# A Flamingo-style two-layer kernel: the second half's router and shared-expert tasks stand one unit later, and the last block of expert weights is split behind the routing-weight chain

## The chip, the cores and the metric

The kernel runs on one core of one Trainium2 chip. The metric is the device time of one execution in microseconds (us). For the kernel before, three timed runs gave 567.09, 568.3 and 570.09 us; the median is 568.3 us. Engines are named as the profile names them: PE (TensorE, matmuls), PEld (its weight loads), DVE (VectorE), ACT (ScalarE), POOL (GpSimd) and SP (SyncE, which issues the DMAs).

## The reference, cut to what matters

Four sub-layers stand one after another on 1024 tokens of width 256. The change touches only the last one, the routed experts:

```python
logits = x @ gate_w.T                       # 32 experts
scores = sigmoid(logits); sb = scores + gate_bias
# groups of 8 experts: the two best groups stay, then the 8 best experts of those
wsel = wsel / wsel.sum(-1, keepdims=True) * 2.5          # routing weights cw
x_lat = x @ fc1_w.T                                      # 256 -> 128
h = relu2(einsum('tl,eil->eti', x_lat, w1)) * cw.T[:, :, None]
y_lat = einsum('eti,eli->tl', h, w2)
routed = y_lat @ fc2_w.T
shared = relu2(x @ shared_up_w.T) @ shared_down_w.T
out = x_in + tanh(g_ffn[1]) * (shared + routed)
```

## The kernel before, in words

Every product is computed as three matmuls (lo by hi, hi by lo, hi by hi), so that every operand exists as a "hi" tile, a rounded copy that ACT writes, and a "lo" tile, the remainder that DVE or POOL subtracts. Whatever feeds PE therefore passes through ACT and then DVE or POOL.

The 1024 tokens are two halves of 512. The experts run as 64 units, `i` from 0 to 63: units 0 to 31 are the 32 experts on the first half of the tokens, 32 to 63 the same experts on the second half. In unit `i` PE runs `down(i)` and then `up(i + 4)`, a "pair" of six 128x512 matmuls. Between `up` and `down` of one unit DVE multiplies relu by the row of routing weights (`root`, tile `e_r`), ACT squares it (`expert_square`, tiles `e_hi` and `e_sq` or a PSUM bank), and DVE or POOL subtracts (`expert_low`, tile `e_lo`). POOL takes the subtraction in units 1, 3, 6, 8, 10, 12, 27, 29 and 31 of the first half.

While the first half's experts run, the second half's normalisation, router, latent projection and shared expert are computed by single "tasks", each put ahead of one unit's pair by the table `TASK_IN_UNIT`. `N` transposes one 128-row chunk of the normalised tokens `h` (two tasks; ACT then writes `hT_hi`, DVE `hT_lo`), `L` computes the logits (24 matmuls of 32 columns), `X` the latent projection, `U` a quarter of the shared expert's up projection (four tasks), `C` transposes the finished routing weights `cw`. All tasks use PSUM bank 1, so each waits until the one before it has been read out (`wait_taken`). The order on every engine is the order in which the code issues it; nothing reorders it. The places of the router's own steps are written as unit numbers too: `scores_of_experts`, `best_of_groups`, `best_experts`, `weight_sum` on DVE, and `biased`, `mask_groups`, `choose`, `roots_begin`, `roots_step`, `roots_end` on POOL. Together they make the chain from `L` to `C`; `roots_end` writes `cw` and signals `cw_ready`.

Expert weights arrive in blocks of 4 experts (128x1024). SP loads a block, ACT copies its hi part (`block_high`, placed by `UNIT_OF_BLOCK`), POOL subtracts its lo part (`block_low`, placed by `LOW_UNIT_OF_BLOCK`), and PE waits for `blk_done` ahead of the first `up` that uses it. Block 28 serves experts 12 to 15, block 29 experts 16 to 19, block 30 experts 20 to 23, block 31 experts 24 to 27 and block 32, the last, experts 28 to 31 (tiles `ex_hi1`, `ex_lo1`); so `up(28)`, which stands in unit 24, needs block 32.

After `C` the weights go through ACT (`cwT`) to DRAM and come back as rows (`store_weights`, `load_row`) for the second half's `root(32)` and on.

Of the kernel before, what the change touches and what calls it, by code (L numbers as in the profile page):

```python
# [5 lines left out]
def flamingo_two_layer_kernel(nc, x, ids, ctx_t, g_xattn, g_ffn, w_gate_t, w_up_t, w_down_t,  # L6
# [19 lines left out]
    NG = 2  # L26
# [11 lines left out]
    SC = SI // P  # L38
# [11 lines left out]
    with ctx:  # L50
# [169 lines left out]
        for q in (2, 3):  # L220
# [81 lines left out]
                  ("K", 3), ("V", 3), ("S", 0), ("D", 0)] + [("E", q) for q in range(E // 4)]  # L302
        STEP_OF_BLOCK = {0: 10, 1: 11, 2: 12, 3: 13, 4: 14, 5: 15, 7: 16, 8: 17, 9: 18, 11: 19, 12: 20, 13: 21, 15: 22,
                         22: 23, 24: 24, 27: 25, 30: 26, 31: 27}
        UNIT_OF_BLOCK = {0: 28, 6: 29, 7: 30, 10: 31, 16: 32}
        LOW_UNIT_OF_BLOCK = {1: 28, 6: 29, 7: 30, 10: 31, 16: 32}
        LOAD_AT_ROW = {4: 29, 8: 30, 13: 31, 16: 32}


        TASK_IN_STEP = {"m11": ("M", 0), "e11": ("M", 1), "e22": ("N", 0), "m23": ("N", 1), "e23": ("L", 0), "m24": ("X", 0),  # L310
                        "e24": ("U", 0), "m25": ("U", 1), "e25": ("U", 2), "m26": ("U", 3), "e30": ("C", 0)}
        TASK_IN_UNIT = {6: ("N", 0), 8: ("N", 1), 10: ("L", 0), 11: ("X", 0), 13: ("U", 0), 15: ("U", 1), 17: ("U", 2), 19: ("U", 3),
                        23: ("C", 0)}
        SHARED_DOWN = {3: (0, 0), 4: (0, 1), 5: (0, 2), 9: (0, 3), 61: (1, 0), 62: (1, 1), 63: (1, 2)}


# [246 lines left out]
        def _(pool):  # L563
# [96 lines left out]
            def shared_low(n):  # L660
                pool.wait_ge(su_taken, n + 1)
                nc.gpsimd.tensor_tensor(s_lo[:, n % SC, :], s_sq[:, n % 2, :], s_hi[:, n % SC, :].bitcast(F32), ALU.subtract)\
                    .then_inc(s_done, 1)
# [67 lines left out]
            def roots_step():  # L731
                own(newton(cwv[:, :], cwy[:, :], cwt[:, :]))

            def roots_end():
                G.tensor_tensor(cw_flat, cw_flat, cwy[:, :], ALU.mult).then_inc(cw_ready, 1)
# [49 lines left out]
            for i in range(NI):  # L785
                expert_low(i + 2)
                if i == 3:
                    norm_factors(1, 3)
                elif i == 11:
                    biased(1)  # L790
                elif i == 13:
                    mask_groups(1)
                elif i == 15:
                    choose(1)
                elif i == 17:
                    roots_begin(1)
                    roots_step()
                elif i == 18:
                    roots_step()
                elif i == 19:  # L800
                    roots_step()
                    roots_end()
                if i in (15, 17, 19, 21):
                    shared_low(SC + (i - 15) // 2)
                if i in LOW_UNIT_OF_BLOCK:
                    block_low(LOW_UNIT_OF_BLOCK[i])

        @block.scalar
        def _(act):
# [245 lines left out]
            for i in range(NI):  # L1055
                expert_square(i + 3)
                if i in TASK_IN_UNIT:
                    take_task(1, TASK_IN_UNIT[i], 1)
                if i in (15, 17, 19, 21):
                    shared_high(SC + (i - 15) // 2)  # L1060
                if i == E + 1:
                    act.wait_ge(down_done, E)
                    nc.scalar.activation(yl_hi[0][:, :], ps[:, 0, :], ACT.Copy).then_inc(yl_hi_done, 2)
                if i in UNIT_OF_BLOCK:
                    block_high(UNIT_OF_BLOCK[i])
# [6 lines left out]
        def _(dve):  # L1072
# [426 lines left out]
                if i >= 1:  # L1499
                    expert_low(i - 1)  # L1500
            for i in range(NI):
                if i in (7, 9):
                    norm_chunk_low(1, (i - 7) // 2, 1, 2 * NG + 4 + (i - 7) // 2)
                elif i == 12:
                    latent_low(1, 1)
                elif i in (14, 16, 18, 20):
                    shared_relu(SC + (i - 14) // 2, 1)
                root(i + 3)
                expert_low(i + 2)
                if i == 0:  # L1510
                    add_attention(GN)
                    add_attention(GN + 1)
                elif i == 1:
                    add_attention(GN + 2)
                    add_attention(GN + 3)
                    count(GN)
                    count(GN + 1)
                elif i == 2:
                    count(GN + 2)
                    own(count(GN + 3))  # L1520
                    aggregate(1)
                elif i == 4:
                    normalise(2, range(GN, GN + 2))
                elif i == 5:
                    normalise(2, range(GN + 2, NT)).then_inc(h_ready, 1)
                elif i == 11:
                    scores_of_experts(1)
                elif i == 12:
                    best_of_groups(1, range(GN)).then_inc(gtop_done, 1)
                elif i == 15:  # L1530
                    best_experts(1)
                elif i == 17:
                    weight_sum(1)
                elif i == E + 2:
                    routed_low(0, 0)
                    routed_low(0, 1)
                elif i == E + 5:
                    add_result(0)
                    add_result(1)
                elif i == E + 6:  # L1540
                    add_result(2)
                    add_result(3)
# [530 lines left out]
```

## Time and profile before

| what | value |
|---|---|
| timed runs | 567.09, 568.3, 570.09 us; median 568.3 us |
| profiled execution, its own time | 568.33 us |
| its span | 566.5 us |
| PE busy | 537.0 us, 95% of the span |
| DVE, ACT, POOL busy | 389.8, 350.9, 320.5 us |
| granted TensorE clock, mean | 0.994 of full speed |

The profiled execution took as long as the median run. Its span, first to last instruction, is 1.8 us shorter than its time. All times below that are points in time are microseconds from the span's start. The stretch that the change touches is 440 to 516 us.

### The profile page before, as it was taken

How to read it: one execution, taken by the hardware profiler on the slowest of the kernel's cores; microseconds unless marked ns; L12 is line 12 of the kernel's file. 1: busy time of each engine (PE TensorE's matmuls, PEld its weight loads, DVE VectorE, ACT ScalarE, POOL GpSimd, SP SyncE). 2: the span in 40 equal slices, each digit the busy share in tenths (PEclk: the TensorE clock that was granted, in tenths of full speed). 3: DMA queues.
4: the chain of work that ended last, by engine and by line, in shares of the span. 5: the costliest groups of instructions: out<-in, count | busy, mean ns of one | idle time of the engine just before them, and what ended most of it. 6: DMA issues, size and time to landing. Idle time of an engine off the chain costs nothing.

```text
span 566.5 us, 9626 instructions
## 1 busy us (share of the span) xinstructions
PE 537.0 (95%) x3240; PEld 462.2 (82%) x3240; DVE 389.8 (69%) x822; ACT 350.9 (62%) x723; POOL 320.5 (57%) x320
## 2 busy tenths in 40 slices
PE   3999998998999999999999999999999989999997
PEld 3877766777778988999999999989998878777786
DVE  4867988689956575656655576646665757878883
ACT  3651155666478676766757565745757665777882
POOL 2579137999348797655544424426698465762220
PEclk9999999999999999999999999989999998999999
DMA  8901136510057768677696768534354735356651
GB/s 278 357 23 46 47 111 185 189 38 1 20 185 226 222 186 261 218 247 224 217 289 191 244 206 229 188 98 163 115 189 149 241 125 174 112 146 189 217 178 39
DMA packets 66672, 95.78 MB, mean 169 GB/s; under 512 B 6336, under 2 KB 38848, under 8 KB 66624
## 3 DMA queue, kind: packets, MB, share of 16 engines
q1 hardware_dynamic: 66624, 95.17, 53.0%
q8 instruction: 27, 0.44, 0.3%
q14 instruction: 21, 0.17, 0.1%
HBM read 67.23 MB, written 27.92 MB: 168 GB/s over the span
## 4 chain that ended last, share of the span: by engine, by line
PE 69%; DVE 11%; POOL 6%; ACT 5%; issue 4%; DMA 3%; SPq 1%; DVEq 0%; POOLq 0%
PE ps L1557 20%; PE ps L1558 19%; PE ps L1559 19%; PE ps L1662 4%; PE ps L1767 2%; PE ps L1751 2%; DMA k_hl<-k_scratch 1%; DVE e_r L1472 1%; PE ps L1774 1%; DMA blk_raw<-in_w_blocks 1%; DVE qtok L1223 1%; ACT q2T L921 1%; PE ps L1780 1%; DMA cw_row<-cw_scratch 1%; DVE e_lo L1482 1%
## 5 line engine op out<-in xcount | busy, mean ns | idle before, releaser
L657 POOL TENSOR_TENSOR probs<-probs,rsum 128x512 f32<-128x512 f32 x64 | 66.4, 1041 | 60.5 <-DVE rsum L1252 60.4
L1247 DVE TENSOR_REDUCE nmax<-ps 128x2 f32<-128x512 f32 x64 | 44.0, 688 | 35.6 <-PE ps L1559 35.3
L959 ACT ACTIVATE probs<-ps,nmax 128x256 f32<-128x256 f32 x128 | 59.7, 481 | 1.6 <-DVE nmax L1247 1.4
L578 POOL TENSOR_TENSOR kv_w_lo<-blk_raw,kv_w_hi 128x1024 fp32r<-128x1024 f32 x16 | 38.9, 2431 | 37.2 <-ACT kv_w_hi L826 37.2
L1045 ACT ACTIVATE e_hi<-e_r 128x512 fp32r<-128x512 f32 x64 | 40.2, 629 | 30.4 <-DVE e_r L1472 29.6
L1472 DVE SCALAR_TENSOR_TENSOR e_r<-ps,cw_row 128x512 f32<-128x512 f32 x64 | 43.6, 684 | 12.8 <-PE ps L1559 10.3
L1238 DVE TENSOR_TENSOR pT_lo<-ps,pT_hi 128x512 fp32r<-128x512 f32 x64 | 43.7, 685 | 11.9 <-ACT pT_hi L965 11.4
L780 POOL TENSOR_TENSOR e_lo<-e_sq,e_hi 128x512 fp32r<-128x512 f32 x19 | 24.5, 1292 | 45.1 <-ACT e_sq L1051 42.6
L1243 DVE TENSOR_TENSOR oT_lo<-ps,oT_hi 128x512 fp32r<-128x512 f32 x32 | 22.1, 691 | 40.2 <-ACT oT_hi L969 40.2
L965 ACT ACTIVATE pT_hi<-ps 128x512 fp32r<-128x512 f32 x64 | 38.3, 600 | 15.9 <-PE ps L1662 15.8
L969 ACT ACTIVATE oT_hi<-ps 128x512 fp32r<-128x512 f32 x32 | 19.1, 597 | 40.8 <-PE ps L1559 40.8
L584 POOL TENSOR_TENSOR k_hl<-k_hl 128x512 fp32r<-128x512 f32 x18 | 23.8, 1322 | 32.1 <-ACT k_hl L894 32.1
L1662 PE MATMUL ps<-eye,probs 128*128 128x128 f32 x256 | 39.0, 275 | 1.6 <-DVE kv_out L1278 1.0
L837 ACT ACTIVATE kv_hi<-ps 128x512 fp32r<-128x512 f32 x38 | 22.9, 602 | 26.9 <-PE ps L1559 26.9
L1557 PE MATMUL ps<-pT_hi,v_hl 128*128 128x256 f32 x128 | 36.6, 286 | 1.1 <-DVE pT_lo L1238 0.5
L1557 PE MATMUL ps<-k_hl,qT_lo 128*128 128x256 f32 x128 | 37.3, 292 | 0.0
L1559 PE MATMUL ps<-k_hl,qT_hi 128*128 128x256 f32 x128 | 36.4, 285 | 0.0
L1558 PE MATMUL ps<-k_hl,qT_hi 128*128 128x256 f32 x128 | 36.3, 284 | 0.0
L1559 PE MATMUL ps<-wo_hi,oT_hi 128*128 128x256 f32 x128 | 36.2, 283 | 0.0
L1558 PE MATMUL ps<-wo_lo,oT_hi 128*128 128x256 f32 x128 | 36.2, 283 | 0.0
L1557 PE MATMUL ps<-wo_hi,oT_lo 128*128 128x256 f32 x128 | 36.2, 283 | 0.0
L1559 PE MATMUL ps<-pT_hi,v_hl 128*128 128x256 f32 x128 | 36.2, 282 | 0.0
(299 smaller groups left out, 1876.9 us busy)
## 6 DMA issues: line engine op xcount, KB each, us to landing
cw_row<-cw_scratch SPq DMA_DIRECT2D x64, 256.0 KB, 3.6
v_hl<-v_scratch SPq DMA_DIRECT2D x24, 512.0 KB, 3.6
blk_raw<-in_w_blocks SPq DMA_DIRECT2D x23, 512.0 KB, 4.4
k_scratch<-kv_out SPq DMA_DIRECT2D x32, 256.0 KB, 2.6
v_scratch<-kv_out SPq DMA_DIRECT2D x32, 256.0 KB, 3.2
k_hl<-k_scratch SPq DMA_DIRECT2D x14, 512.0 KB, 3.5
v_scratch<-kv_hi SPq DMA_DIRECT2D x24, 256.0 KB, 2.8
blk_raw<-in_w_tail SPq DMA_DIRECT2D x10, 512.0 KB, 4.6
```

Of the source, the lines that this page charges most:

```text
L578: nc.gpsimd.tensor_tensor(lo[:, :], blk_raw[j % 2][:, :], hi[:, :].bitcast(F32), ALU.subtract).then_inc(blk_done, 1)
L657: nc.gpsimd.tensor_tensor(probs[:, b, :, :], probs[:, b, :, :], rsum[:, b, :].unsqueeze(2).to_broadcast([P, 2, S]), ALU.mult).then_inc(pro ...
L959: last = nc.scalar.activation(probs[:, b, t, :], ps[:, S_BANK[b], t * S:(t + 1) * S], ACT.Exp, bias=nmax[:, b, t:t + 1], accum_out=esum[:, ...
L965: nc.scalar.activation(pT_hi[:, b, :, :].rearrange("p k q -> p (k q)"), ps[:, P_BANK[b], :], ACT.Copy).then_inc(p_hi_done, 1)
L1045: nc.scalar.activation(e_hi[i % 4][:, :], e_r[i % 2][:, :], ACT.Square).then_inc(e_hi_done, 1)
L1238: V.tensor_tensor(pT_lo[:, b, :, :].rearrange("p k q -> p (k q)"), ps[:, P_BANK[b], :], pT_hi[:, b, :, :].rearrange("p k q -> p (k q)").bi ...
L1247: V.tensor_reduce(nmax[:, b, :], ps[:, S_BANK[b], :].rearrange("p (t k) -> p t k", t=2), AX.X, ALU.max, negate=True).then_inc(max_done, 1)
L1472: V.scalar_tensor_tensor(e_r[i % 2][:, :], ps[:, UP_BANK[i % 4], :], 0.0, cw_row[i % 4][:, :], ALU.max, ALU.mult).then_inc(root_done, 1)
L1557: mm(dst, l_lo, r_hi, start=first, stop=False, **kw)
L1558: mm(dst, l_hi, r_lo, start=False, stop=False, **kw)
L1559: return mm(dst, l_hi, r_hi, start=False, stop=last, **kw)
L1662: last = nc.tensor.transpose(ps[:, P_BANK[b], k * S + t * P:k * S + (t + 1) * P], probs[:, b, t, k * P:(k + 1) * P], ident)
```

## The change: all second-half tasks one unit later, block 32 at unit 20

Every entry of `TASK_IN_UNIT` moves up by one unit, and with it each engine's share of these tasks: ACT's copies, DVE's and POOL's router steps, the shared expert's relu, square and subtraction. The blocks 28 to 31 keep their units. Block 32's ACT copy and POOL subtraction move from unit 16 to unit 20, which on POOL is from between `choose` and `roots_begin` to behind `roots_end`. The number of instructions is the same.

```diff
-        UNIT_OF_BLOCK = {0: 28, 6: 29, 7: 30, 10: 31, 16: 32}
-        LOW_UNIT_OF_BLOCK = {1: 28, 6: 29, 7: 30, 10: 31, 16: 32}
+        UNIT_OF_BLOCK = {0: 28, 6: 29, 7: 30, 10: 31, 20: 32}
+        LOW_UNIT_OF_BLOCK = {1: 28, 6: 29, 7: 30, 10: 31, 20: 32}
...
-        TASK_IN_UNIT = {6: ("N", 0), 8: ("N", 1), 10: ("L", 0), 11: ("X", 0), 13: ("U", 0), 15: ("U", 1), 17: ("U", 2), 19: ("U", 3),
-                        23: ("C", 0)}
+        TASK_IN_UNIT = {7: ("N", 0), 9: ("N", 1), 11: ("L", 0), 12: ("X", 0), 14: ("U", 0), 16: ("U", 1), 18: ("U", 2), 20: ("U", 3),
+                        24: ("C", 0)}
...
@@ POOL @@
-                elif i == 15:
+                elif i == 16:
                     choose(1)
-                elif i == 17:
+                elif i == 18:
                     roots_begin(1)
-                    roots_step()
-                elif i == 18:
                     roots_step()
                 elif i == 19:
                     roots_step()
+                elif i == 20:
+                    roots_step()
                     roots_end()
-                if i in (15, 17, 19, 21):
-                    shared_low(SC + (i - 15) // 2)
+                if i in (16, 18, 20, 22):
+                    shared_low(SC + (i - 16) // 2)
                 if i in LOW_UNIT_OF_BLOCK:
                     block_low(LOW_UNIT_OF_BLOCK[i])
...
@@ ACT @@
-                if i in (15, 17, 19, 21):
-                    shared_high(SC + (i - 15) // 2)
+                if i in (16, 18, 20, 22):
+                    shared_high(SC + (i - 16) // 2)
...
@@ DVE @@
-                if i in (7, 9):
-                    norm_chunk_low(1, (i - 7) // 2, 1, 2 * NG + 4 + (i - 7) // 2)
-                elif i == 12:
+                if i in (8, 10):
+                    norm_chunk_low(1, (i - 8) // 2, 1, 2 * NG + 4 + (i - 8) // 2)
+                elif i == 13:
                     latent_low(1, 1)
...
-                elif i == 15:
+                elif i == 16:
                     best_experts(1)
-                elif i == 17:
+                elif i == 18:
                     weight_sum(1)
```

On ACT, this is what stands around the first transposed chunk before. `kv_w_hi0` is the hi copy of block 29, `wo_hi3` that of block 30, `e_hi2` and `e_sq0` the squares of unit 10, `e_hi0` and `e_sq0` further down those of unit 12, `hT_hi` the copies of the two chunks:

```order
L1047 ACTIVATE ps<-e_r1 128x512
L973 ACTIVATE hT_hi<-ps 128x512
L826 ACTIVATE kv_w_hi0<-blk_raw1 128x1024
L1045 ACTIVATE e_hi2<-e_r0 128x512
L1051 ACTIVATE e_sq0<-e_r0 128x512
L826 ACTIVATE wo_hi3<-blk_raw0 128x1024
L1045 ACTIVATE e_hi3<-e_r1 128x512
L1047 ACTIVATE ps<-e_r1 128x512
L973 ACTIVATE hT_hi<-ps 128x512
```

And the same place on ACT after the change:

```order
L1047 ACTIVATE ps<-e_r1 128x512
L826 ACTIVATE kv_w_hi0<-blk_raw1 128x1024
L1045 ACTIVATE e_hi2<-e_r0 128x512
L1051 ACTIVATE e_sq0<-e_r0 128x512
L973 ACTIVATE hT_hi<-ps 128x512
L826 ACTIVATE wo_hi3<-blk_raw0 128x1024
L1045 ACTIVATE e_hi3<-e_r1 128x512
L1047 ACTIVATE ps<-e_r1 128x512
L1045 ACTIVATE e_hi0<-e_r0 128x512
L1051 ACTIVATE e_sq0<-e_r0 128x512
L973 ACTIVATE hT_hi<-ps 128x512
```

Block 29's copy and the squares of unit 10 have moved ahead of the first chunk's copy, and the squares of unit 12 ahead of the second's, since the tasks moved by a unit and the blocks did not.

On POOL, the difference at the routing chain. `wsel` ends `choose`, the first `cw` row is the begin of `roots_begin`, the last is `roots_end`; `ex_lo1` is the lo part of block 32, `s_lo` the shared expert's:

```order
 L723 TENSOR_TENSOR wsel<-sel,sc 128x128
 L662 TENSOR_TENSOR s_lo<-s_sq,s_hi 128x512
-L578 TENSOR_TENSOR ex_lo1<-blk_raw0,ex_hi1 128x1024
 L727 TENSOR_TENSOR cw<-wsel,wden 128x128
...
 L735 TENSOR_TENSOR cw<-cw,cwy 128x128
-L662 TENSOR_TENSOR s_lo<-s_sq,s_hi 128x512 x2
+L662 TENSOR_TENSOR s_lo<-s_sq,s_hi 128x512
+L578 TENSOR_TENSOR ex_lo1<-blk_raw0,ex_hi1 128x1024
+L662 TENSOR_TENSOR s_lo<-s_sq,s_hi 128x512
```

The block's subtraction has left the middle of the chain and stands behind its end, with one `s_lo` between them.

## Rows read from the trace of the kernel before

**Rows 1.** The page: busy time of each engine, and the chain that ended last.

```profile
PE 537.0 (95%) x3240; PEld 462.2 (82%) x3240; DVE 389.8 (69%) x822; ACT 350.9 (62%) x723; POOL 320.5 (57%) x320
...
PE 69%; DVE 11%; POOL 6%; ACT 5%; issue 4%; DMA 3%; SPq 1%; DVEq 0%; POOLq 0%
```

**Rows 2.** Timeline of PE, units 6 to 10: start, duration, instruction, [idle before].

```profile
459.23 0.63 PE L1870 MATMUL ps<-eye,h 128*128 128x128 f32 x4 [1.75 <-DVE h L1271]
...
461.07 0.39 PE L1557 MATMUL ps<-e_hi,wq_lo 128*128 128x512 f32 x1
...
462.43 0.60 PE L1870 MATMUL ps<-eye,h 128*128 128x128 f32 x4
...
464.25 0.28 PE L1557 MATMUL ps<-wq_hi,s_lo 128*128 128x256 f32 x1
...
465.67 0.40 PE L1557 MATMUL ps<-e_hi,wo_lo 128*128 128x512 f32 x1
...
467.16 0.25 PE L1557 MATMUL ps<-gw_hi,hT_lo 128*128 128x32 f32 x1
```

**Rows 3.** Timeline of ACT, the same stretch, and the copy of the routing weights.

```profile
460.26 0.58 ACT L1047 ACTIVATE ps<-e_r 128x512 f32<-128x512 f32 x1
460.78 0.58 ACT L973 ACTIVATE hT_hi<-ps 128x512 fp32r<-128x512 f32 x1
461.25 1.05 ACT L826 ACTIVATE kv_w_hi<-blk_raw 128x1024 fp32r<-128x1024 f32 x1
462.71 0.63 ACT L1045 ACTIVATE e_hi<-e_r 128x512 fp32r<-128x512 f32 x1 [0.41 <-DVE e_r L1472]
...
501.49 0.26 ACT L996 ACTIVATE cwT<-ps 128x128 f32<-128x128 f32 x1
```

**Rows 4.** Timeline of DVE: hT_lo, both halves' last wden step, a late row.

```profile
418.49 0.16 DVE L1326 SCALAR_TENSOR_TENSOR wden<-wden 128x4 f32<-128x4 f32 x1
...
461.39 0.69 DVE L1284 TENSOR_TENSOR hT_lo<-ps,hT_hi 128x512 fp32r<-128x512 f32 x1 [1.71 <-ACT hT_hi L973]
...
487.55 2.32 DVE L1326 SCALAR_TENSOR_TENSOR wden<-wden 128x4 f32<-128x4 f32 x1
...
510.49 0.69 DVE L1472 SCALAR_TENSOR_TENSOR e_r<-ps,cw_row 128x512 f32<-128x512 f32 x1 [0.29 <-DMA cw_row<-cw_scratch]
```

**Rows 5.** Timeline of POOL: blocks 29 and 32, e_lo, the chain's end.

```profile
462.38 2.40 POOL L578 TENSOR_TENSOR kv_w_lo<-blk_raw,kv_w_hi 128x1024 fp32r<-128x1024 f32 x1 [2.00 <-ACT kv_w_hi L826]
...
467.25 1.28 POOL L780 TENSOR_TENSOR e_lo<-e_sq,e_hi 128x512 fp32r<-128x512 f32 x1
...
487.45 2.40 POOL L578 TENSOR_TENSOR ex_lo<-blk_raw,ex_hi 128x1024 fp32r<-128x1024 f32 x1 [0.43 <-ACT ex_hi L826]
489.95 0.40 POOL L727 TENSOR_TENSOR cw<-wsel,wden 128x128 f32<-128x128 f32 x1
...
498.52 0.45 POOL L735 TENSOR_TENSOR cw<-cw,cwy 128x128 f32<-128x128 f32 x1
498.94 2.54 POOL L662 TENSOR_TENSOR s_lo<-s_sq,s_hi 128x512 fp32r<-128x512 f32 x2
```

**Rows 6.** Timeline of PE, units 19, 22, 23, 24, 32 and 34.

```profile
490.52 0.50 PE L1557 MATMUL ps<-hT_hi,kv_w_lo 128*128 128x512 f32 x1 [0.91 <-DVE s_sq L1297]
...
496.73 0.50 PE L1557 MATMUL ps<-e_hi,wo_lo 128*128 128x512 f32 x1 [0.44 <-DVE e_lo L1482]
...
499.12 0.30 PE L1894 MATMUL ps<-eye,cw 128*128 128x128 f32 x1 [0.74 <-POOL cw L735]
...
501.34 0.39 PE L1557 MATMUL ps<-xl_hi,ex_lo 128*128 128x512 f32 x1
...
512.22 0.47 PE L1557 MATMUL ps<-e_hi,wq_lo 128*128 128x512 f32 x1 [0.51 <-DVE e_lo L1482]
...
515.29 0.50 PE L1557 MATMUL ps<-e_hi,wq_lo 128*128 128x512 f32 x1
```

**Rows 7.** Busy time by stretch (PE, PEld, DVE, ACT, POOL), granted clock, DMA.

```profile
471.00:474.00 3.00, 3.00 (x9) 2.35 (x8) 1.99 (x4) 1.46 (x3) 2.38 (x1) 0.50 0.62 236
```

More of the change, by code:

```diff
@@ L788, in _ @@
                     norm_factors(1, 3)
-                elif i == 11:
+                elif i == 12:
                     biased(1)
-                elif i == 13:
+                elif i == 14:
                     mask_groups(1)
-                elif i == 15:
+                elif i == 16:
                     choose(1)
-                elif i == 17:
+                elif i == 18:
                     roots_begin(1)
-                    roots_step()
-                elif i == 18:
                     roots_step()
@@ L1501, in _ @@
             for i in range(NI):
-                if i in (7, 9):
-                    norm_chunk_low(1, (i - 7) // 2, 1, 2 * NG + 4 + (i - 7) // 2)
-                elif i == 12:
+                if i in (8, 10):
+                    norm_chunk_low(1, (i - 8) // 2, 1, 2 * NG + 4 + (i - 8) // 2)
+                elif i == 13:
                     latent_low(1, 1)
-                elif i in (14, 16, 18, 20):
-                    shared_relu(SC + (i - 14) // 2, 1)
+                elif i in (15, 17, 19, 21):
+                    shared_relu(SC + (i - 15) // 2, 1)
                 root(i + 3)
@@ L1525, in _ @@
                     normalise(2, range(GN + 2, NT)).then_inc(h_ready, 1)
-                elif i == 11:
+                elif i == 12:
                     scores_of_experts(1)
-                elif i == 12:
+                elif i == 13:
                     best_of_groups(1, range(GN)).then_inc(gtop_done, 1)
-                elif i == 15:
+                elif i == 16:
                     best_experts(1)
-                elif i == 17:
+                elif i == 18:
                     weight_sum(1)
```

## The prediction, made before the changed kernel ran

> **What bounds the kernel now.** I read the page first. PE is busy 95% of the span and holds 69% of the chain that ended last [rows 1], so a change that leaves PE's work alone can only win or lose PE's gaps. I then read PE's timeline through the stretch in which the tasks stand, looking for the bracketed idle times, and behind each gap the timelines of the engines that feed it.
>
> Six gaps stand there. PE waits 1.75 us for the normalised tokens ahead of the first transpose [rows 2]. It waits 0.91 us ahead of the fourth shared task, 0.44 ahead of `down(22)`, 0.74 ahead of the weights' transpose `C`, and 0.51 ahead of `down(32)` [rows 6]. A sixth, smaller one stands ahead of `down(34)`. Each bracket costs about 0.15 us more, since PE restarts that long after its releaser: `cw` ends at 498.97, `C` starts at 499.12 [rows 5, 6]. What the change can reach at all is thus 5 to 6 us, about 1% of the kernel.
>
> **Units.** A pair costs PE 1.36 us (461.07 to 462.43), shared down with four column groups 1.42 (464.25 to 465.67) [rows 2]; a transposed chunk 0.36. I compare both kernels at equal PE work. A task that comes one unit later has one more pair behind it, so 1.36 us come off.
>
> **First transpose, -1.4.** `h` is ready on DVE at the same time as before, because nothing ahead of it moved: the transpose starts at 459.23 in both [rows 2]. Before, PE stood still; now `down(6)` and `up(10)` fill 1.36 us of that. Both can run: their inputs come from units that are long done. About 0.5 us of waiting is left.
>
> **Second transpose, +1.8.** It shares bank 1 with the first and so waits for `hT_lo` of chunk 0. Before, ACT copied that chunk at 460.78, right behind the squares of unit 9, and DVE's `hT_lo` came at 461.39 [rows 3, 4]; the second transpose at 462.43 did not wait [rows 2]. Now ACT does two things ahead of the copy. Block 29's copy starts at 460.8 and takes 1.05. The squares of unit 10 follow; `up(10)` ends about 458.9 (459.23 - 1.75 + 1.36) and DVE's row of unit 10 takes 0.69 behind it, done by 460.3, so they wait for nothing, and take 0.54 + 0.62, 1.15 together (the bounds of these two are the 0.63 and 0.58 rows). The copy then runs 462.8 to 463.4, `hT_lo` (0.69) 463.4 to 464.1, and the transpose starts at 464.25. PE arrives at 462.43, as before, since two pairs stand between the transposes in both. So 1.8 us of new wait. Queued behind it are shared down and pair 9, and nothing else of PE's can pass.
>
> **`down(10)` and the logits, +1.1.** From 464.25 PE does the chunk, shared down and pair 9 and is at `down(10)` at 467.4. POOL's `e_lo(10)` stands behind the lo parts of blocks 29 and 30. Block 29 runs 461.9 to 464.3 (2.40 each [rows 5]). Block 30's hi copy on ACT now follows the chunk, 463.4 to 464.4, so its lo part runs 464.4 to 466.8, `e_lo(10)` (1.28) to 468.05; PE continues at 468.2. That is +0.75. Before, `e_lo(10)` came at 467.25 as well [rows 5], but the logits stood ahead of `down(10)` and covered it: the cover is gone. The second chunk's copy now stands behind the squares of unit 12, the second of which waits for `e_lo(10)` to free its buffer: 468.1, +0.6, copy to 469.2, `hT_lo` to 469.9, logits at 470.05. PE arrives at 469.55, so 0.5 more, less the 0.1 of before: +0.4. Together the logits start 2.9 us later than at 467.16 [rows 2], with 1.36 of work more done: **+1.5** so far.
>
> **The routing chain, -2.1.** From the logits to `C` the same steps stand beside the same pairs, with one piece taken out. DVE's last step of `weight_sum` on 128x4 numbers took 2.32 us, while the identical instruction in the first half took 0.16 [rows 4]. It ended (489.87) as POOL's lo part of block 32 ended (487.45 + 2.40), and POOL's own chain went on at 489.95 [rows 5]. With block 32 gone from there I expect 0.16, that is 2.16 us less in the chain. `cw` was complete at 498.97; now at 498.97 + 2.9 - 2.16 = 499.7. PE was ready for `C` at 499.12 - 0.89 = 498.23. It loses the wait for the fourth shared task (1.06, its relu stood on DVE behind the held step) and the one at `down(22)` (0.59), so it arrives at 498.23 + 2.9 - 1.65 = 499.5, and `C` starts at 499.85, held by `cw` alone. Against 499.12, and with one pair more done, PE is 0.6 ahead; that is 2.1 gained since the logits.
>
> In the Trainium skill, SBUF — State Buffer, the section on its ports, a DVE instruction with two SBUF inputs and a POOL instruction that reads SBUF exclude each other for the whole instruction, whichever starts first. That would be the mechanism of the row of 2.32 us, and it speaks for a gain, but also for a danger: the step now comes at about 490.6, near the end of POOL's first `s_lo` (about 488.6 to 489.9 by the shift). If they met, the rule would hold it for up to another 1.3 us, and the sum of this edit would be -0.8 instead of -2.1. The sum here goes by the first half's row.
>
> **Block 32, +2.8.** POOL comes to it behind `cw` and one `s_lo` (half of the 2.54 us of rows 5): 499.7 + 1.25, then 2.40, ready at 503.3, and `up(28)` can start at 503.45. Before, block 32 was done at 489.85, 11.5 us ahead of its use at 501.34 [rows 5, 6]. From `C` to `up(28)` PE has only `down(24)` now: 2.22 us before, less a pair, 0.86. It arrives at 500.7 and waits 2.75. The spare time of the block was spent and more. `up(28)` starts 2.1 us later than before at equal work.
>
> **Behind it, -1.0.** Between `up(28)` (501.34) and `down(34)` (515.29) stand 9.5 pairs, 12.92 us, in 13.95 [rows 6]: 1.0 us of waiting. It comes from the round trip of the weights: `cwT` ends at 501.75, and DVE's second row of the new half is released by its DMA at 510.49, 8.7 us later [rows 3, 4]. With `C` 0.7 later the rows come by 511.2, `down(32)` can run at 512.9, and PE, 2.1 later, gets there at 513.6. The rest of the kernel is copied unchanged.
>
> **Sum.** -1.4 + 1.8 + 1.1 - 2.1 + 2.8 - 1.0 is +1.2, by the times themselves +2.1 - 1.0 = +1.1. The profiled execution took 568.33 us, the median of the runs 568.3, so I forecast **569.4 us**. That is within 0.5% (2.8 us, 565.5 to 571.1), about what a measurement of this kernel can tell from no change.
>
> **Rivals.**
> - *The held step is not POOL's doing* (slower). If the 2.32 us come from something in the chain's own surroundings and stay, `cw` comes at 501.85, block 32 is ready at 505.5, and `up(28)` runs at 505.6, 4.3 later than before; less 1.0 it is 568.33 + 3.3 = **571.6**. Against it: the first half's 0.16 with POOL idle, and the two ends within 0.02 us. It decides from a hold of about 1.7 us on. Chance 0.09.
> - *The second transpose does not wait* (faster). If ACT gets to the chunk's copy in time, the new waits of 1.8 and 1.1 fall away, the chain ends at 498.97 + 1.3 - 2.16 = 498.1, block 32 at 501.7, `up(28)` 0.5 later than before, and most of the 1.0 is kept: **567.8**. Against it: ACT's order is fixed, and block 29's data was there by 461.25 before without a wait [rows 3]. Chance 0.08.
> - *Block 32 is in time* (no new wait of 2.8). Then the trip of the weights takes over: `C` is 0.7 later, so `down(32)` is at best 0.6 later than 512.22: **568.9**. It is hidden anyway, and so the cheap mistake. Chance 0.05.
> - *The clock.* In 471 to 474 PE ran at half clock, 1.2 GHz, granted 0.50 [rows 7], behind the logits, whose small matmuls start at 467.16 [rows 2]. 3 us at half clock do the work of 1.5, so it costs 1.5 us. I assume it again. Without it PE is earlier at `C`, but `C` waits for `cw`, so 0 to 1.5 are saved: **568.2** in the middle. With the new waits right ahead of the logits nothing speaks for its absence. Chance 0.2.
>
> In the Trainium skill, TensorE: Matmul & The Clock Gate, Part 1, the gate's window is free-running and does not start with the kernel. By that rule the stretch at half clock may fall away or appear in any execution of either kernel, whatever the change does, and the two medians can differ by 1.5 us for no cause in the diff; the sum would be 568.2 in such a run and 569.4 in another.
>
> **Chances.** Forecast as worked out 0.58; the four rivals as given. Range 567.4 to 571.6: below lies a share of the clock's case, above the held step. Faster by over 0.5% needs two of the favourable cases at once and a lost stretch of half clock: 0.04. Slower by over 0.5% is the held step and some unseen wait: 0.10. Within: 0.86.
>
> **What would show it.** In the changed kernel's PE timeline: the first transpose with a wait under 0.6 us; the second with 1.6 to 2.0, released by DVE's `hT_lo`; `down(10)` released by POOL, 0.7; no wait ahead of the fourth shared task; `C` with 0.2 to 0.5; `up(28)` with 2.5 to 3, released by POOL's `ex_lo`; none at `down(32)`. On DVE, the last `wden` step under 0.3 us. The forecast is wrong if that step stays long, if the second transpose doesn't wait, or if `up(28)` doesn't.

## The result and the profile after

The changed kernel takes 570.64 us (median of 20 runs, 568.1 to 571.88) against 567.92 (median of 20, 567.09 to 570.46). The ratio is 1.0041, 95% interval 1.0031 to 1.005 (it is worked out over the runs and is not the quotient of the two medians, which is 1.0048): it is slower by 0.4%, real but inside the 0.5% that the prediction counted as no change. The forecast was 569.4 in 567.4 to 571.6; the loss forecast was 1.1 us, and the one measured is 2.3 by the ratio and 2.7 by the medians. The profiled execution took 570.34 us with a span of 568.5, so 2.0 us more than the one of before in both.

The page of the changed kernel, which answers to [rows 1]: busy times, and the chain that ended last.

```profile
PE 537.3 (95%) x3234; PEld 463.0 (81%) x3240; DVE 387.8 (68%) x822; ACT 351.2 (62%) x723; POOL 320.4 (56%) x320
...
PE 72%; DVE 8%; POOL 7%; ACT 5%; issue 3%; DMA 3%; SPq 1%; DVEq 0%; POOLq 0%; ACTq 0%
```

PE is as busy as before. DVE is 2.0 us less busy, nearly all of it the held `wden` step (2.32 us before, 0.16 now). Nothing here tells where the time went, so the timeline has to.

The timeline of PE in the changed kernel, against [rows 2] and [rows 6] (start, duration, instruction, idle before it and its releaser):

```profile
459.29 0.63 PE L1870 MATMUL ps<-eye,h 128*128 128x128 f32 x4 [0.40 <-DVE h L1271]
...
464.17 0.66 PE L1870 MATMUL ps<-eye,h 128*128 128x128 f32 x4 [1.50 <-DVE hT_lo L1284]
...
468.11 0.50 PE L1557 MATMUL ps<-e_hi,wo_lo 128*128 128x512 f32 x1 [0.47 <-POOL e_lo L780]
...
470.04 0.25 PE L1557 MATMUL ps<-gw_hi,hT_lo 128*128 128x32 f32 x1 [0.25 <-DVE hT_lo L1284]
...
499.88 0.30 PE L1894 MATMUL ps<-eye,cw 128*128 128x128 f32 x1 [0.52 <-POOL cw L735]
...
503.35 0.50 PE L1557 MATMUL ps<-xl_hi,ex_lo 128*128 128x512 f32 x1 [2.47 <-POOL ex_lo L578]
503.68 0.39 PE L1558 MATMUL ps<-xl_lo,ex_hi 128*128 128x512 f32 x1
503.91 0.41 PE L1559 MATMUL ps<-xl_hi,ex_hi 128*128 128x512 f32 x1
504.14 0.60 PE L1557 MATMUL ps<-e_hi,ex_lo 128*128 128x512 f32 x1
504.54 0.63 PE L1558 MATMUL ps<-e_lo,ex_hi 128*128 128x512 f32 x1
504.96 0.63 PE L1559 MATMUL ps<-e_hi,ex_hi 128*128 128x512 f32 x1
```

All six waits stand where the forecast had them, and every start is within 0.12 us of it. Four of the brackets fall just outside what the prediction gave as signs (1.50 for 1.6 to 2.0, 0.47 for 0.7, 0.52 for 0.2 to 0.5, 2.47 for 2.5 to 3). The rows behind the last wait are what the forecast did not have. From the fourth matmul behind it on, the matmuls no longer start 0.23 us apart but 0.42, and each lasts 0.63 instead of 0.39.

Busy time by stretch of the changed kernel (PE, PEld, DVE, ACT, POOL; then the granted clock, DMA share, GB/s), against [rows 7]:

```profile
473.40:476.90 3.50, 3.50 (x10) 2.68 (x9) 1.83 (x4) 1.58 (x4) 1.72 (x1) 0.51 0.11 40
504.40:507.80 3.40, 3.40 (x10) 2.61 (x10) 1.53 (x3) 1.28 (x3) 1.37 (x2) 0.53 0.06 16
```

The kernel before for the same PE work behind `up(28)`:

```profile
501.00:504.00 3.00, 3.00 (x15) 2.48 (x14) 2.43 (x5) 2.85 (x7) 1.40 (x2) 1.00 0.67 170
504.00:508.00 4.00, 4.00 (x20) 3.30 (x19) 2.88 (x5) 3.42 (x7) 1.68 (x2) 1.00 0.24 71
```

The stretch behind the logits was there before too, 2.5 us earlier. The one at 504.4 to 507.8 is new: 10 matmuls in 3.4 us at 0.53, where the kernel before does 15 in 3.0 at 1.00. So the 1.2 GHz level was granted twice in this part of the changed kernel and once before. Each such stretch lowers the mean clock of an execution by 0.003 (1.7 of 567 us). Every profile of this case has one more of them far ahead of the change, so that a profile with one has a mean of 0.997, with two 0.993 or 0.994, with three 0.990 or 0.991.

The rows of ACT, DVE and POOL around the first chunk and the chain's end, one fence each, against [rows 3 to 5]. ACT:

```profile
460.83 1.05 ACT L826 ACTIVATE kv_w_hi<-blk_raw 128x1024 fp32r<-128x1024 f32 x1
461.78 0.61 ACT L1045 ACTIVATE e_hi<-e_r 128x512 fp32r<-128x512 f32 x1
462.30 0.61 ACT L1051 ACTIVATE e_sq<-e_r 128x512 f32<-128x512 f32 x1
462.82 0.57 ACT L973 ACTIVATE hT_hi<-ps 128x512 fp32r<-128x512 f32 x1
```

DVE:

```profile
463.43 0.69 DVE L1284 TENSOR_TENSOR hT_lo<-ps,hT_hi 128x512 fp32r<-128x512 f32 x1 [1.81 <-ACT hT_hi L973]
...
490.45 0.16 DVE L1326 SCALAR_TENSOR_TENSOR wden<-wden 128x4 f32<-128x4 f32 x1
```

POOL:

```profile
499.27 0.46 POOL L735 TENSOR_TENSOR cw<-cw,cwy 128x128 f32<-128x128 f32 x1
499.69 1.30 POOL L662 TENSOR_TENSOR s_lo<-s_sq,s_hi 128x512 fp32r<-128x512 f32 x1
500.93 2.36 POOL L578 TENSOR_TENSOR ex_lo<-blk_raw,ex_hi 128x1024 fp32r<-128x1024 f32 x1
```

ACT has block 29's copy and two squares ahead of the chunk's copy, which starts at 462.82 instead of 460.78. The `wden` step takes 0.16 us instead of 2.32. Block 32 runs from 500.93 to 503.29, and `up(28)` starts 0.06 later.

### The profile page after: what moved, and what is told of

Same layout as the page of the kernel before. It is cut to its first block, busy times and chain, and to the rows that moved or that the text cites. A ratio compares the mean times of both kernels' runs of the same rounds, so it can differ in the third digit from the quotient of the medians.

```text
span 568.5 us, 9620 instructions
## 1 busy us (share of the span) xinstructions
PE 537.3 (95%) x3234; PEld 463.0 (81%) x3240; DVE 387.8 (68%) x822; ACT 351.2 (62%) x723; POOL 320.4 (56%) x320
## 4 chain that ended last, share of the span: by engine, by line
PE 72%; DVE 8%; POOL 7%; ACT 5%; issue 3%; DMA 3%; SPq 1%; DVEq 0%; POOLq 0%; ACTq 0%
PE ps L1557 21%; PE ps L1558 20%; PE ps L1559 20%; PE ps L1662 4%; PE ps L1767 2%; DMA k_hl<-k_scratch 2%; PE ps L1751 2%; POOL kv_w_lo L578 1%; DMA xr<-in_x 1%; PE ps L1774 1%; ACT q2T L921 1%; ACT kv_w_hi L826 1%; PE ps L1780 1%; DVE xr L1200 1%; ACT probs L959 1%
```

## The experiments

Every ratio is to the kernel before, timed beside it on the same chip. Its median was 568.05 us beside e1 to e4, 567.51 beside e5 to e8 and 567.91 beside e9 and e10. Across these three sessions the ratios are compared; they can differ from the quotient of the medians by up to 0.001, or 0.6 us.

### The two halves of the change apart: e1_shift_only and e2_block_only

The first has the shifted tasks and leaves block 32 at unit 16. The second has the tasks of before and moves only the block:

```diff
-        UNIT_OF_BLOCK = {0: 28, 6: 29, 7: 30, 10: 31, 16: 32}
-        LOW_UNIT_OF_BLOCK = {1: 28, 6: 29, 7: 30, 10: 31, 16: 32}
+        UNIT_OF_BLOCK = {0: 28, 6: 29, 7: 30, 10: 31, 20: 32}
+        LOW_UNIT_OF_BLOCK = {1: 28, 6: 29, 7: 30, 10: 31, 20: 32}
```

> The tasks one unit later, block 32 left at unit 16. My theory (the shift costs time at the second transpose and at down(10), the block's move gives back the held step of the routing chain): the logits start 2.9 us later than before as in the changed kernel, the last wden step on DVE takes over 2 us again because POOL's block 32 stands beside it, C comes about 2.4 us later than before, up(28) does not wait, down(32) waits 1.9 us for the rows of weights. In all +1.9 us over the kernel before, 569.8 us. No stretch at half clock behind up(28). Rival (the shift gives its 1.4 us and only the late block costs): 566.5 us, faster than before.

Measured: 568.71 us (12 runs, 567.77 to 569.88), ratio 1.0013 (1.0001 to 1.0025). Nearer to the theory than to the rival, but a microsecond better. The waits of 1.53, 0.48 and 0.26 us ahead of the second transpose, `down(10)` and the logits are there, and `wden` is held again, 1.83 us, until POOL's subtraction of block 32 ends. What the expectation had too dear is `down(32)`: PE waited 0.24 us there, not 1.9. `C` came 1.7 us later than before (500.83) and not 2.4; the stretch behind the logits is missing in this profile.

> The tasks where they were before, only block 32 at unit 20. My theory: the last wden step takes 0.16 instead of 2.32 us, cw is complete 2.2 us earlier, the waits ahead of the fourth shared task (1.06) and down(22) (0.59) go, up(28) waits 1.4 us for the block, the wait at down(32) shrinks from 0.7 to 0.3. In all -1.5 us against before, 566.4 us, with no half clock behind up(28), since the wait is half as long as in the changed kernel. Rival (the block's lateness is the whole loss of the changed kernel, and would be here): 569 us or more.

Measured: 566.95 us (12 runs, 565.32 to 568.58), ratio 0.9977 (0.9964 to 0.9989), a gain of 1.3 us. The theory of a gain stands. `C` starts at 497.22, 1.9 us earlier than before, and the wait at `up(28)` is short. PE in this kernel:

```profile
500.72 0.50 PE L1557 MATMUL ps<-xl_hi,ex_lo 128*128 128x512 f32 x1 [1.12 <-POOL ex_lo L578]
```

No stretch at half clock follows it, and none of the twelve runs had a mean clock under 0.993. The halves don't add: +0.7 and -1.3 us would be -0.6, and together (1.0041) they are +2.3. About half of these 3 us is in a wait: the shift takes one pair of 1.36 us from between `C` and `up(28)`, and 1.12 + 1.36 = 2.48 is the wait measured in the changed kernel. The other half is in no wait; it is about the price of the stretch at half clock, 1.7 us.

### The wait filled with matmuls: e3_filled_wait

The changed kernel, with 12 more matmuls of 128x512 between `down(24)` and `up(28)`. They write into the bank that `up(28)` then overwrites, so their results are not used, and the wait for block 32 stands behind them.

```diff
+                if i == 28:
+                    for _ in range(4):
+                        product(ps[:, UP_BANK[i % 4], :], expert_weights(27, 0)[1], both(xl_hi[g], xl_lo[g], A, A))
+                    pe.wait_ge(blk_done, j + 1)
                 product(ps[:, UP_BANK[i % 4], :], w, both(xl_hi[g], xl_lo[g], A, A)).then_inc(up_filled, 1)
```

> The changed kernel, and PE runs 12 extra matmuls of 512 columns (2.7 us, into the bank that up(28) overwrites, results unused) ahead of its wait for block 32. My theory (1.5 us of the changed kernel's loss is the half clock that follows PE's standstill of 2.6 us at up(28)): up(28) starts at the same 503.4 us, no stretch at half clock follows, 569.1 us, 1.5 us faster than the changed kernel although PE does more. Rival (the half clock has to do with something else, or costs nothing at the end): 570.6 us or, if the extra matmuls push up(28), more.

Measured: 567.74 us (12 runs, 566.54 to 568.78), ratio 0.9985 (0.9974 to 0.9996). A kernel with 2.7 us more of matmuls (12 of 0.23) is faster than the changed one, and by the ratio a little faster than the one before (their medians are 0.3 us apart). PE there, with the last of the extra matmuls, `up(28)` at 502.83 and `up(30)` at 505.65, and then the stretch behind it:

```profile
502.60 0.39 PE L1559 MATMUL ps<-xl_hi,ex_hi 128*128 128x512 f32 x1
502.83 0.45 PE L1557 MATMUL ps<-xl_hi,ex_lo 128*128 128x512 f32 x1
503.11 0.39 PE L1558 MATMUL ps<-xl_lo,ex_hi 128*128 128x512 f32 x1
...
505.65 0.39 PE L1557 MATMUL ps<-xl_hi,ex_lo 128*128 128x512 f32 x1
```

```profile
504.00:508.00 4.00, 4.00 (x19) 3.27 (x19) 2.56 (x5) 3.02 (x6) 2.11 (x2) 1.00 0.08 19
```

`up(28)` starts at 502.83, since block 32 is no earlier. What is gone is the half clock: granted 1.00 in 504 to 508. From `up(28)` to `up(30)` PE takes 2.82 us here (502.83 to 505.65) and 4.44 in both profiles of the changed kernel (the second's rows stand with e7), so the stretch costs 1.6 us. The gain over the changed kernel, 2.7 to 3.2 us (1.0032 and 1.0041 in its two timings, to 0.9985), is more than that. Ten of the twelve runs had a mean granted clock of 0.997, against 0.990 or 0.991 in 16 of the 20 of the changed kernel, and in e3's profile the stretch behind the logits is missing too. If a run at 0.997 has the early stretch, as every profile has, it has neither of the two. This edit stands behind the logits, and no run tells why that stretch was mostly absent.

### The wait lengthened without the shift: e10_block_later

The kernel of e2 with block 32 at unit 21, so that one more `s_lo` stands ahead of it on POOL.

```diff
-        UNIT_OF_BLOCK = {0: 28, 6: 29, 7: 30, 10: 31, 20: 32}
-        LOW_UNIT_OF_BLOCK = {1: 28, 6: 29, 7: 30, 10: 31, 20: 32}
+        UNIT_OF_BLOCK = {0: 28, 6: 29, 7: 30, 10: 31, 21: 32}
+        LOW_UNIT_OF_BLOCK = {1: 28, 6: 29, 7: 30, 10: 31, 21: 32}
```

> The experiment with the block alone moved (566.95 us, PE waited 1.12 us at up(28)), with block 32 at unit 21, behind one more s_lo of 1.28 us. The tasks stay at their places of the kernel before. The wait at up(28) grows to 2.4 us. Theory, a standstill of PE of about 2.5 us is followed by a stretch at half clock of some 3 us: time 567.0 + 1.3 + 1.5 = 569.8, less what slack behind it takes, with a granted clock of 0.5 behind up(28). Rival, the stretch in the changed kernel has to do with the shifted tasks and not with the wait's length: full clock behind up(28), 568.2.

Measured: 569.14 us (12 runs, 567.33 to 570.71), ratio 1.0014 (0.9998 to 1.0031). PE at `up(28)`, and the stretch behind:

```profile
501.48 0.79 PE L1557 MATMUL ps<-xl_hi,ex_lo 128*128 128x512 f32 x1 [2.36 <-POOL ex_lo L578]
```

```profile
502.00:504.00 2.00, 2.00 (x6) 1.54 (x5) 0.69 (x1) 0.11 (x1) 0.90 (x1) 0.50 0.35 104
```

Half clock again, with the tasks where they always were. So the stretch belongs to the wait and not to the shift. By the ratios, 1.24 us more wait cost 2.1 us (0.9977 to 1.0014; the ends of the intervals leave 0.5 to 3.8), where 2.8 were expected for the theory and 1.3 for the rival. So the time alone decides nothing here; the granted clock does. The runs are mixed: six at a mean clock of 0.99 or 0.991 took 569.7 us on average, four at 0.994 to 0.996 took 568.0, and two at 0.993 took 570.2, longer than their clock accounts for.

### ACT's copies ahead of the squares: e4_copies_first

The changed kernel; ACT copies the two transposed chunks ahead of the squares of the same unit, and blocks 30 and 31 move to units 10 and 12.

```diff
-        UNIT_OF_BLOCK = {0: 28, 6: 29, 7: 30, 10: 31, 20: 32}
+        UNIT_OF_BLOCK = {0: 28, 6: 29, 10: 30, 12: 31, 20: 32}
...
             for i in range(NI):
+                ahead = i in TASK_IN_UNIT and TASK_IN_UNIT[i][0] == "N"
+                if ahead:
+                    take_task(1, TASK_IN_UNIT[i], 1)
                 expert_square(i + 3)
-                if i in TASK_IN_UNIT:
+                if i in TASK_IN_UNIT and not ahead:
                     take_task(1, TASK_IN_UNIT[i], 1)
```

> The changed kernel with ACT's two copies of transposed chunks ahead of the squares of the same unit, and blocks 30 and 31 at units 10 and 12 instead of 7 and 10. My theory (the new waits at the second transpose and at down(10) are ACT's and POOL's order): the second transpose waits 0.8 instead of 1.7 us, down(10) and the logits don't wait, the logits start at 467.6 instead of 470.0 us, C is 2.3 us earlier, up(28) waits the same 2.6 us behind C and the half clock follows as before: 568.3 us, 2.3 us faster than the changed kernel. Rival (PE would be held at C or at up(28) anyway, so the earlier waits are free): 570.6 us.

Measured: 568.51 us (566.8 to 570.12, 12 runs), ratio 1.0008 (0.9994 to 1.0022), as the theory had it. PE in this kernel:

```profile
462.57 0.66 PE L1873 MATMUL ps<-eye,h 128*128 128x128 f32 x4 [0.46 <-DVE hT_lo L1287]
...
500.65 0.50 PE L1560 MATMUL ps<-xl_hi,ex_lo 128*128 128x512 f32 x1 [2.46 <-POOL ex_lo L578]
```

The second transpose waits 0.46 instead of 1.50, the waits at `down(10)` and the logits are gone, and some 2 us come back (1.0041 to 1.0008). The wait at `up(28)` is the same 2.46, and half clock follows it here too.

### The held step: e5_one_input and e9_no_scale

Two readings of the 2.1 us that the routing chain gained were open: POOL's block 32 held DVE's last `wden` step, or the block only stood in POOL's queue ahead of the chain's next step, and the held step cost nothing. Both kernels are the one before, with this line changed in one and removed in the other (there the reciprocal ahead of it gives the signal, and the weights are left without the factor 2.5):

```diff
-                V.scalar_tensor_tensor(wden[:, :], wden[:, :], ROUTED_SCALE - 1.0, wden[:, :], ALU.mult, ALU.add).then_inc(wden_done, 1)
+                V.tensor_scalar(wden[:, :], wden[:, :], ROUTED_SCALE, None, ALU.mult).then_inc(wden_done, 1)
```

> The kernel before with the last step of weight_sum on DVE written with one SBUF input (tensor_scalar, times 2.5) instead of two; POOL's block 32 stays beside it. Theory of the held input (POOL's subtraction keeps DVE's second SBUF input for its whole length): the step takes about 0.2 instead of 2.32 us, the wait ahead of the fourth shared task (1.06 us) goes. Whether that shortens the routing chain separates two readings. If the held step was what delayed the chain, cw is complete 2.2 us earlier and the kernel gains 1.3 us as with block 32 moved: 566.7 us. If POOL itself is the delay, because block 32 stands in its queue ahead of roots_begin until 489.85 us whatever DVE does, cw stays at 499.0 us, PE waits longer at down(22) and C, and the time is the kernel before's less 0.2: 567.9 us. I expect the second.

Measured: 567.24 us (12 runs, 566.72 to 569.82), ratio 0.9998 (0.9985 to 1.0012). This one tells nothing apart, since the form with one input is held just as long. DVE there:

```profile
486.72 0.18 DVE L1325 RECIPROCAL wden<-wden 128x4 f32<-128x4 f32 x1
486.93 2.30 DVE L1326 TENSOR_SCALAR wden<-wden 128x4 f32<-128x4 f32 x1
```

> The kernel before, with the last step of the sum of weights left out in both halves (the weights are not multiplied by 2.5; the part left out is this scaling). DVE then hands over the reciprocal at 487.5 instead of 489.87. Theory, POOL's queue holds the chain: block 32's subtraction still stands ahead of POOL's first cw step and still ends at about 489.85, so cw and C come as before (C within 0.3 us of 499.12 at equal clock), only PE's wait of 0.91 ahead of the fourth shared task goes, and C's wait grows by as much; time 568, the same within 0.3 us. Rival, the held step holds the chain: POOL's cw step comes by about 2 us earlier, C at 497 to 498, time 566.3.

Measured: 567.9 us (10 runs, 567.08 to 569.8), ratio 0.9997 (0.998 to 1.0015), as the first theory had it. POOL and PE in this kernel:

```profile
486.88 2.41 POOL L578 TENSOR_TENSOR ex_lo<-blk_raw,ex_hi 128x1024 fp32r<-128x1024 f32 x1 [0.43 <-ACT ex_hi L826]
489.24 0.41 POOL L727 TENSOR_TENSOR cw<-wsel,wden 128x128 f32<-128x128 f32 x1
```

```profile
496.04 0.50 PE L1556 MATMUL ps<-e_hi,wo_lo 128*128 128x512 f32 x1 [1.98 <-DVE e_lo L1481]
498.46 0.30 PE L1893 MATMUL ps<-eye,cw 128*128 128x128 f32 x1 [0.76 <-POOL cw L735]
```

DVE has the reciprocal of the weights' sum ready at 486.95 and goes on with its other work at once. POOL takes the first `cw` step at 489.24 all the same, behind block 32, and `C` stands as far behind block 32 as before (11.58 us from the block's start, 11.67 in [rows 5, 6]). PE arrives early and waits 1.98 ahead of `down(22)` instead. The profile of e5, which has full clock behind the logits as this one does, is the nearest to hold it against: with the step held for 2.30 us, block 32 starts on POOL at 486.83 and `C` at 498.50; without the step, at 486.88 and 498.46. So the chain was held by POOL's queue; the held step on DVE cost nothing that shows (by e9's interval, -1.1 to +0.9 us).

### The changed kernel once more: e7_after_again

No edit; timed beside e5, e6 and e8.

> The changed kernel once more, unaltered, so that the kernels of this job and the one with the filled wait can be held against it on the same kind of chip. My theory (its loss is its own, and half of it is a stretch at half clock behind up(28)): 570.6 us, 2.5 us slower than before, half clock behind up(28) in the profile. Rival (the two kernels differ by where the stretches at half clock happen to fall in a set of executions, so the difference is no property of the change): anything between 568 and 570.6 us, with fewer such stretches than in the first 20 runs.

Measured: 569.1 us (12 runs, 566.93 to 571.27), ratio 1.0032 (1.0017 to 1.0048). The waits are those of the first profile to 0.02 us (2.48 at `up(28)`), but for `C`, where PE waited 0.74 instead of 0.52. Half clock follows `up(28)` again, but it was absent behind the logits. Nine of the runs had a mean clock of 0.993 or 0.994 and took 569.1 on average, two had 0.991 and took 570.6, and one had 0.996 and took 566.9. The 14 runs of the kernel before at 0.993 or 0.994 in the same session took 567.9: with as many stretches at half clock the two kernels are 1.2 us apart, about what the forecast had for the waits alone. The two medians of the changed kernel, 570.64 and 569.1, differ by the share of its executions that ran at the lower mean clock. PE at `up(28)` and `up(30)`:

```profile
502.13 0.50 PE L1557 MATMUL ps<-xl_hi,ex_lo 128*128 128x512 f32 x1 [2.48 <-POOL ex_lo L578]
...
506.57 0.39 PE L1557 MATMUL ps<-xl_hi,ex_lo 128*128 128x512 f32 x1
```

### What the experiments point to: e8_order_only and e6_filled_and_ordered

e8 is the kernel before with ACT's copies ahead of the squares, as in e4, and the blocks 30, 31 and 32 at units 9, 11 and 19. e6 also moves a shared down task of before's into PE's first wait:

```diff
-        SHARED_DOWN = {3: (0, 0), 4: (0, 1), 5: (0, 2), 9: (0, 3), 61: (1, 0), 62: (1, 1), 63: (1, 2)}
+        SHARED_DOWN = {3: (0, 0), 4: (0, 1), 5: (0, 2), 6: (0, 3), 61: (1, 0), 62: (1, 1), 63: (1, 2)}
...
             for i in range(NI):
+                if i == 6:
+                    shared_down(*SHARED_DOWN[i])
                 if i in TASK_IN_UNIT:
```

> As the version before, without the moved shared down: PE stands 1.75 us ahead of the first transpose again. My theory (filled waits count fully, since nothing behind them is bound by another engine until C): 1.4 us slower than with it, 565.6 us. Rival (PE's wait at C takes the gain back): the same time as with it.

> A version that takes what the runs pointed to: tasks in the units of the kernel before, the last quarter of the first half's shared down at unit 6 ahead of the first transpose (it fills 1.4 us of the 1.75 us wait there), ACT's copies of the transposed chunks ahead of the same unit's squares, blocks 30, 31 and 32 at units 9, 11 and 19. My theory: the waits at the first transpose (1.4 of 1.75), ahead of the logits, of the fourth shared task and of down(22) go, up(28) waits 1.4 us, down(32) does not wait. In all -3.9 us against before: 564.1 us. Rival (the routing chain is the bound from the tokens on, so filling PE's wait ahead of it changes nothing): 566.5 us as with block 32 moved alone.

Measured: e8 565.62 us (12 runs, 564.81 to 566.85), ratio 0.9967 (0.9952 to 0.9981), and e6 564.17 us (6 runs, 562.06 to 565.45), ratio 0.9938 (0.9918 to 0.9959), both as expected. PE in e6:

```profile
459.13 0.63 PE L1873 MATMUL ps<-eye,h 128*128 128x128 f32 x4 [0.32 <-DVE h L1274]
...
497.81 0.50 PE L1560 MATMUL ps<-xl_hi,ex_lo 128*128 128x512 f32 x1 [1.11 <-POOL ex_lo L578]
```

```profile
499.00:502.00 3.00, 3.00 (x15) 2.48 (x14) 2.25 (x4) 2.21 (x4) 1.26 (x2) 1.00 0.21 54
```

The first wait is filled by 1.42 us of work that has to be done anyway, without moving the tasks. Block 32 is out of the chain, and the wait for it of 1.11 us is followed by full clock. e6 beats both kernels: it is 3.3 us under the one before and 4.9 under the changed one, timed beside it (569.1).

## Why the prediction was nearly right

The time fell into the range and the kernel was slower, as forecast. Five of the six terms held in size. The sixth had its wait right and its price too low by the stretch at half clock behind it.

One reading was wrong and did no harm. The prediction adds 0.15 us to every bracket because PE restarts that long after its releaser. A bracket runs from the end of the matmul before to the restart, so it holds the restart already. What it leaves out is that each matmul lasts 0.39 us while the next one starts 0.23 behind it, so that PE could have gone on 0.16 earlier than the bracket begins. The last matmul before the first transpose, in the kernel before, ends at 457.48, and 1.75 behind that is 459.23:

```profile
457.09 0.39 PE L1559 MATMUL ps<-xl_hi,wo_hi 128*128 128x512 f32 x1
```

- **First transpose, -1.4.** Held: start 459.29 (459.23 forecast, equal to before), 0.40 us of wait left.
- **Second transpose, +1.8.** Held: it starts at 464.17, 464.25 forecast, released by `hT_lo`. The copy came at 462.82 (462.8 forecast). e4 shows the cause, since with the copy moved up most of the wait goes.
- **`down(10)` and the logits, +1.1.** Held: 468.11 and 470.04, forecast 468.2 and 470.05.
- **The routing chain, -2.1.** The size held: `C` at 499.88, forecast 499.85. The reason was half right. The prediction took the 2.16 us out as the held step's; e9 shows that the block's place in POOL's queue held the chain, and that the step without it gains nothing. Both leave with the block, so the number was the same, by luck and not by the reasoning. The rival by which the step stays held (571.6) was not what happened, for the step took 0.16. The danger that it meets `s_lo` did not come true either.
- **Block 32, +2.8. This is the step that failed, by its size.** The wait was right (503.35 and 2.47 us, forecast 503.45 and 2.75). Its price was not. Compared at equal work, PE is 2.01 us behind the kernel before at `up(28)` (503.35 against 501.34) and 3.72 behind it two pairs later, at `up(30)` (the first row of each fence below). The 1.7 us between are the stretch at half clock. `C` starts at 499.88 and PE would be at `up(28)` 0.86 later, so the wait with its restart cost 2.6, and with the stretch the term is about +4.3. The prediction treated the clock as a matter of the logits only and asked what could remove a stretch, not what a standstill of 2.5 us in front of full load could add. In all four profiles with a wait of 2.4 to 2.5 us there (the changed kernel's two, e4, e10) half clock follows it, in e3, where the wait is filled, it does not, and in the three with a wait of 1.1 us (e2, e6, e8) it does not. PE takes 4.30 to 4.45 us from `up(28)` to `up(30)` in the four and 2.82 to 2.87 in the others.
- **Behind it, -1.0.** Held: eight pairs on, at `up(38)`, the 3.72 have shrunk to 2.57 (the second row of each fence), and no wait is left at `down(32)`. A further 0.55 comes back by the end: between 534.6 and 538.1 the kernel before falls back by about 0.5, most of it in a short wait at 537.7 that the changed kernel's profile does not have. The changed kernel's second profile has such a wait itself (0.42 at 536.67, released by DVE's `e_lo`), so this part differs between executions of one kernel and is not counted for the change. So the profiled times differ by +2.0 where +1.1 was forecast: the half clock's 1.7, less these 0.55 and the small errors of the other terms.

PE before, at `up(30)` and `up(38)`:

```profile
504.07 0.39 PE L1557 MATMUL ps<-xl_hi,ex_lo 128*128 128x512 f32 x1
...
516.10 0.39 PE L1557 MATMUL ps<-xl_hi,wq_lo 128*128 128x512 f32 x1
```

The same two in the changed kernel:

```profile
507.79 0.39 PE L1557 MATMUL ps<-xl_hi,ex_lo 128*128 128x512 f32 x1
...
518.67 0.39 PE L1557 MATMUL ps<-xl_hi,wq_lo 128*128 128x512 f32 x1
```

The rivals: the second transpose did wait, and block 32 was not in time, so 567.8 and 568.9 are out. The rival of the clock, a missing stretch behind the logits, happens in single executions (e7's profile), but there too the stretch behind `up(28)` came in addition. Its sum was also wrong: 0 to 1.5 off 569.4 is 568.65 in the middle and not 568.2. And little of the stretch is hidden by the wait for `cw`: from the second transpose to `C` e7 takes 34.35 us and the first profile 35.71, so 1.36 are saved.

In the Trainium skill, TensorE: Matmul & The Clock Gate, Part 1, the gate's window is free-running. By that rule a wait of a given length brings the half clock in some executions and not in others. For a wait of 2.1 us the profiles agree. Ahead of 90.1 to 90.6 us, in code that no edit touches, PE stands still for 2.1 us in all twelve. In five of them half clock follows at 91 us, and in all five it comes back behind the logits. In the other seven the clock stays at its upper level there and falls at 375 us instead, and only one of the seven (the kernel before) has the stretch behind the logits as well. Busy time 2 us behind that wait, in the kernel before:

```profile
92.00:94.00 2.00, 2.00 (x10) 1.69 (x9) 1.93 (x7) 0.90 (x2) 0.43 (x1) 1.00 0.00 0
```

The same in the changed kernel:

```profile
92.00:94.00 2.00, 2.00 (x6) 1.51 (x6) 1.93 (x7) 0.56 (x2) 0.32 (x1) 0.50 0.00 0
```

For the wait of 2.4 to 2.5 us no profile shows the half clock missing, and four are too few to say that it always comes. The single runs fit stretches that come and go: those of the changed kernel take 571.0 us on average at 0.990 or 0.991 (16 runs) and 569.1 at 0.993 or 0.994 (four). Which of the stretches was missing in the four is not known.

Still open is why the stretch behind the logits was mostly missing in e3, and why it comes with the early one at 91 us.

## What to carry to other kernels

A wait of PE has two prices, its length and the half clock that may follow it. Here one wait of 2.5 us cost 4.2 to 4.3 with the stretch behind it, while those of 1.1 were followed by full clock. When an item is moved out of a chain, work out from the timeline how far ahead of its use it lands, and fill a wait with work that depends on nothing (e6) rather than shift a row of tasks past the copies that they wait for. Where an instruction is shown as held, look at what stood in the queue of the engine that waits for it before crediting the hold with any time (e9).

## What the hardware showed that I had not expected

- Twelve unused matmuls in front of a wait made the changed kernel 2.7 to 3.2 us faster (e3, ratio 0.9985 against 1.0032 and 1.0041). They filled 2.47 us in which PE stood still anyway, and the clock stayed at its upper level behind them. That is worth 1.6 us; the rest is about what a missing stretch behind the logits saves (1.36, e7), and the edit does not explain why that one was missing.
- A DVE instruction of 128x4 numbers lasts 2.3 us while POOL subtracts 128x1024, in the form with two SBUF inputs (2.32, [rows 4]) and in the one with one (2.30, e5). Not every step of that size is held. In e1 POOL's subtraction starts at 489.15, ahead of all three steps of `weight_sum`; the sum and the reciprocal, with one input each, take 0.28 and 0.18 inside of it, and only the third step is held, until POOL ends (491.56):

DVE in e1:

```profile
489.23 0.28 DVE L1324 TENSOR_REDUCE wden<-wsel 128x4 f32<-128x128 f32 x1
489.54 0.18 DVE L1325 RECIPROCAL wden<-wden 128x4 f32<-128x4 f32 x1
489.75 1.83 DVE L1326 SCALAR_TENSOR_TENSOR wden<-wden 128x4 f32<-128x4 f32 x1
```

POOL in e1:

```profile
489.15 2.41 POOL L578 TENSOR_TENSOR ex_lo<-blk_raw,ex_hi 128x1024 fp32r<-128x1024 f32 x1
```

In the Trainium skill, SBUF — State Buffer, the section on the two separate sides, DVE shares a port pair with POOL in its 2-port modes as well as with two SBUF inputs, and the loser waits for the whole instruction. The rows of 2.32 and 2.30 us agree: each step ended within 0.02 us of POOL's instruction (489.87 and 489.85, 489.23 and 489.21).
